# A decoder layer's expert stage: the input rows spread by transfers inside SBUF and turned by VectorE in 32x32 blocks, instead of turned by TensorE

## The reference, cut to what matters

```
logits = x @ router_weight.T + router_bias
top_val, top_idx = jax.lax.top_k(logits, 4)          # 4 of 16 experts for each token
gate_up = x @ gate_up_proj[e] + gate_up_proj_bias[e]  # 512 -> 512 gate, 512 up
gate = min(gate, 7); up = clip(up, -7, 7)
glu = gate * sigmoid(1.702 * gate)
out_e = ((up + 1) * glu) @ down_proj[e] + down_proj_bias[e]
out = sum over the 4 experts of weight * out_e;  x = layernorm(x + out)
```

## Time and profile before

| what | us |
|---|---|
| median of 3 runs (1515.5 to 1519.87) | 1516.45 |
| the profiled execution's own time | 1519.72 |
| its span, from the first to the last instruction | 1518.0 |
| PE busy | 1417.6 (93%) |
| DVE, ACT, POOL busy | 949.6, 725.7, 864.8 |
| the experts, from the first turned row to the last product | about 700 |

### The profile page before, as it was taken

How to read it: one execution, slowest core, us unless ns; L and a number is a source line. 1 busy time by engine, 2 the same in 40 slices (tenths; PEclk the granted TensorE clock), 3 DMA queues, 4 the chain that set the end, 5 groups by cost and what they waited for, 6 DMA issues and landing times. The chain is left out here.

```text
span 1518.0 us, 26960 instructions
## 1 busy us (share of the span) xinstructions
PE 1417.6 (93%) x7502; PEld 1016.7 (67%) x7502; DVE 949.6 (63%) x1425; ACT 725.7 (48%) x1405; POOL 864.8 (57%) x712
## 2 busy tenths in 40 slices
PE   6999999889999999998959999999999999999992
PEld 5878888534444444443347888888888888888882
DVE  2334234777888788789875655565656565656564
ACT  4212221268777877876624424444444444354233
POOL 4435342545586577655558456676667586377522
PEclk9999999989999999999869999999999999999996
DMA  5301003464666666571147456666656577375455
GB/s 200 92 22 52 14 26 49 75 111 66 114 118 90 134 130 91 121 128 46 67 160 213 102 125 161 168 163 157 166 142 169 135 202 171 71 195 141 73 129 173
DMA packets 93407, 180.84 MB, mean 119 GB/s; under 512 B 19064, under 2 KB 21880, under 8 KB 92248
## 3 DMA queue, kind: packets, MB, share of 16 engines
q1 hardware_dynamic: 73800, 133.04, 35.3%
q0 software_dynamic: 18320, 45.59, 16.0%
q10 hardware_dynamic: 1152, 0.52, 0.2%
HBM read 116.04 MB, written 33.47 MB: 98 GB/s over the span
## 5 line engine op out<-in xcount | busy, mean ns | idle before, releaser
L952 DVE TENSOR_REDUCE stage<-ps_a 128x2 f32<-128x1024 f32 x256 | 300.0, 1217 | 71.2 <-PE ps_a L1301 70.6
L750 ACT ACTIVATE probs<-ps_b 128x512 f32<-128x512 f32 x504 | 274.3, 596 | 51.6 <-PE ps_b L1316 47.0
L2090 POOL TENSOR_TENSOR we_split<-we_raw,we_split 128x512 f32 (+1 forms) x192 | 248.8, 1535 | 75.8 <-ACT we_split L2081 74.2
L2484 PE MATMUL ps_y<-we_split,hT 128*128 x900 | 226.2, 400 | 2.7 <-issue 1.6
L2484 PE MATMUL ps_u<-we_split,xT 128*128 x900 | 226.1, 400 | 0.0
L2484 PE MATMUL ps_g<-we_split,xT 128*128 x900 | 218.6, 392 | 0.5 <-POOL we_split L2090 0.5
L2484 PEld LDWEIGHTS ps_g<-we_split,xT 128*128 128x128 f32 x900 | 170.0, 189 | 36.3 <-issue 0.9
L2484 PEld LDWEIGHTS ps_y<-we_split,hT 128*128 128x128 f32 x900 | 164.7, 190 | 34.9 <-issue 3.4
L2230 POOL DMA_INDIRECT scratch_acc<-x_keep,to_rows x75 | 119.6, 1594 | 117.1 <-issue 64.2
L2484 PEld LDWEIGHTS ps_u<-we_split,xT 128*128 128x128 f32 x900 | 163.5, 188 | 32.8
L2290 ACT ACTIVATE hT<-ps_h 128x512 fp32r<-128x512 f32 x75 | 44.7, 595 | 292.8 <-PE ps_h L2456 292.8
(11 more groups left out here) (353 smaller groups left out, 2198.9 us busy)
## 6 DMA issues: line engine op xcount, KB each, us to landing
we_raw<-in_w_expert SPq DMA_DIRECT2D x180, 256.0 KB
stack<-xT_raw SPq DMA_DIRECT2D x192, 128.0 KB, 5.5
we_bias<-in_b_expert SPq DMA_DIRECT2D x16, 768.0 KB, 4.6
stage<-in_w SPq DMA_DIRECT2D x5, 1024.0 KB, 5.3
xT_raw<-in_xT SPq DMA_DIRECT2D x4, 1024.0 KB, 6.8
x_tok<-in_x POOLq DMA_DIRECT2D x16, 256.0 KB, 3.0
stage<-in_ctx SPq DMA_DIRECT2D x7, 512.0 KB, 5.5
late<-o_pair SPq DMA_DIRECT2D x112, 32.0 KB
```

What stands on the lines that cost most here:

```text
L750: nc.scalar.activation(probs[:, n % 3, h], src[:], ACT.Exp, scale=DH ** -0.5).then_inc(b_kept, 1)
L952: nc.vector.tensor_reduce(out[:, :, i, k % NC], ps_a[i][:], AX.X, ALU.max, negate=True).then_inc(a_kept[i], 1)
L2090: nc.gpsimd.tensor_tensor(lo, W["raw"][:, k, c], hi, ALU.subtract).then_inc(W["lo"], 1)
L2484: mm = nc.tensor.matmul(out[:], left[:, a, c], w[:, bass.ds(par, 1), k, b, c].squeeze(1), start=(n == 0), stop=(n == len(passes) - 1))
```

## The change

The rows of a tile are no longer turned by PE. ACT issues four transfers inside SBUF for each tile (`move_rows`): transfer q takes columns 128q to 128q+127 of all 128 gathered rows and writes them to the 32 partitions from 32q, four rows of 128 numbers to a partition. One VectorE instruction (`turn_x`) then turns every 32x32 block of that. The result holds the same numbers as a full transpose, but with the 512 input features in another order over (partition, chunk), so the weights of gate and up are loaded in that order too (`weight_rows`). `x_hi` and `x_lo` read the turned rows from SBUF, with a step, instead of from PSUM. PSUM bank `ps_x` and four instructions of PE for each tile go. The buffers for the final layer norm move to make room. Expert 0's weights come in 12 transfers instead of 3.

```diff
-                sp.dma_start(W["raw"][:, k], A["w_expert"][0][:, k]).then_inc(W["loaded"][k], 16)
+                for c in range(KC):
+                    sp.dma_start(W["raw"][:, k, c], weight_rows(A, 0, k, c)).then_inc(W["loaded"][k], 16)
...
+def weight_rows(A, e, k, c):
+
+    if k == 2:
+        return A["w_expert"][e][:, k, c]
+    return A["w_expert"][e][32 * c:32 * c + 32, k].rearrange("a q d -> q a d")
...
-            sp.dma_start(W["raw"][:, k, c], A["w_expert"][e][:, k, c]).then_inc(W["loaded"][k], 16)
+            sp.dma_start(W["raw"][:, k, c], weight_rows(A, e, k, c)).then_inc(W["loaded"][k], 16)
...
-    act.wait_ge(W["loaded"][k], 16 * KC * e + 16)
+    act.wait_ge(W["loaded"][k], 16 * KC * e + 16 * KC)
...
+        moved_rows, turned_rows = [x[:, U + i] for i in range(2)], x[:, U + 2]
+        by_quarter = turned_rows.rearrange("p (g c b) -> p c b g", g=4, c=KC)
...
-                nc.scalar.activation(xT[:, j % 2, 0], four(ps_x), ACT.Copy).then_inc(xT_hi, 1)
+                nc.scalar.activation(by_row(xT[:, j % 2, 0]), by_quarter, ACT.Copy).then_inc(xT_hi, 1)
+
+            def move_rows(i, j):
+                act.wait_ge(gathered[j], 16 * (i // U) + 16)
+                if i >= 2:
+                    act.wait_ge(x_turned, i - 1)
+                for q in range(4):
+                    act.dma_start(moved_rows[i % 2][32 * q:32 * q + 32, :], x_rows[j][:, q * P:q * P + P]).then_inc(
+                        moved[i % 2], 16)
...
             for j in range(2):
+                move_rows(j, j)
+            for j in range(2):
                 x_hi(j, j)
...
                 if i < TILES - 3:
                     aim_from(i + 3, (j + 3) % U)
+                if i < TILES - 2:
+                    move_rows(i + 2, (i + 2) % U)
                 new = act.value_load(pick(G["new"], i), min_val=0, max_val=1)
...
-                nc.vector.tensor_tensor(xT[:, j % 2, 1], four(ps_x), xT[:, j % 2, 0], ALU.subtract).then_inc(xT_lo, 1)
+                nc.vector.tensor_tensor(by_row(xT[:, j % 2, 1]), by_quarter, by_row(xT[:, j % 2, 0]),
+                                        ALU.subtract).then_inc(xT_lo, 1)
+
+            def turn_x(i):
+                dve.wait_ge(moved[i % 2], 64 * (i // 2) + 64)
+                if i > 0:
+                    dve.wait_ge(xT_lo, i)
+                nc.vector.transpose(turned_rows, moved_rows[i % 2]).then_inc(x_turned, 1)
...
                 nc.vector.scalar_tensor_tensor(h[:], ps_u[:], 1.0, glu[:], ALU.add, ALU.mult).then_inc(h_made, 1)
+                if i < TILES - 2:
+                    turn_x(i + 2)
                 if not is_at(i, 0):
                     finish(i - 1, (j - 1) % U)
...
-                if not (isinstance(i, int) and i >= TILES - 2):
-                    turn_x(i + 2, (j + 2) % U)
                 if not is_at(i, 0):
                     down(i - 1)
```

More of the change, by code:

```diff
@@ L2128, in bank @@
             return ctx.enter_context(nc.psum_tensor(name, [P, D], F32))
-        ps_g, ps_u, ps_x, ps_h, ps_y = bank("ps_g"), bank("ps_u2"), bank("ps_x"), bank("ps_h"), bank("ps_y")
+        ps_g, ps_u, ps_h, ps_y = bank("ps_g"), bank("ps_u2"), bank("ps_h"), bank("ps_y")
         from_set, to_set = sem("from_set"), sem("to_set")
@@ L2140, in experts @@
         added, weight_kept = sem("added"), sem("weight_kept")
[L2141 removed]
+        moved = [sem("moved0"), sem("moved1")]
+        final_step = sem("final_step")
         pair_loaded = [sem(f"pair_loaded{g}") for g in range(PAIRS)]
```

28 lines of the change are left out of this document (12 added, 16 removed).

## The result

The changed kernel takes **1735.22 us** (median of 4 runs, 1727.22 to 1744.02) against 1517.09 for the kernel before on the same chip: ratio 1.143, 95% interval 1.140 to 1.147. The prediction had the direction (slower, 0.91), but 1646 us and a range that ended at 1720. The profiled execution took 1732.96 us, with a span of 1731.3.

The account below looks back on a forecast made before the run. In the experts PE alone was taken to set the pace. Terms -26 + 91 + 34 + 31 = +130 on the profiled 1519.7 gave 1649.7, forecast as 1646 us against the runs' median; own range 1600 to 1700 (0.55), overall range 1570 to 1720.

Parts of the forecast that it names:

- Removed: -26 us: PE's row in each tile: one of two 0.35 us pieces goes, 75 times, -26 us; a tile takes 8.77 us.
- An ordinary tile pays 0: Ordinary tile: turn, later x_hi and four issues on ACT still let down start at 8.55, due 8.77; cost 0.
- Where an expert begins: 6.2 us: First three downs of an expert late by 2.1, 2.2 and 1.9 us, at 14 later beginnings and partly the first: +91 us.
- Its first part: First down of an expert: ACT's three weight copies start 2.6 us later behind x_hi, delaying h; 2.1 us lost.
- the other two: Second and third down of an expert: ACT waits for later gathers ahead of its issues and h; 2.2 and 1.9 us.
- The loads: +34 and +31: Gate and up loads on four DMA engines: +34 us for the first tile, +31 us at later experts.
- The second term: Later experts: loads last 43.4 us, so experts of 3 tiles lack 10.4 us and those of 4 lack 1.6; +31 us.
- x_lo against POOL: x_lo with both inputs in SBUF and POOL shut each other out; third down 2.2 us later, 1677 us; left out of sum.
- the first (1729 us): Rival: four engines are full everywhere, so the later-load term is 137 us; +213, 1729 us; chance 0.15.
- The second (moved rows late, 1691): Rival: moved rows land late and DVE waits before finish and x_hi; 0.6 us times 75, +45, 1691 us; chance 0.10.
- The third's 1586 us: Rival: all 16 engines carry gate and up, so nothing is late later; +70, 1586 us; chance 0.13.

Follow-up runs that it names:

- the kernel before with narrow loads: Kernel before, TensorE still turning rows, only gate and up loaded four rows outermost, then 32, as in the change: 1592.55 us.
- with x_lo out of the way: DVE writes turned rows to PSUM, where x_hi and x_lo read them: 1738.70 us against the changed kernel, 1605.25 with gate and up loaded 128 rows outermost.
- wide loads: Changed kernel with gate and up rows laid out by the host so their loads have 128 rows outermost again: 1669.88 us.
- the third buffer's kernel: Third moved-rows buffer added to wide loads, PSUM turned rows, gathers four tiles ahead, spread copies, moves behind h's cut: 1523.22 us; 1600.96 with four-engine loads.

## Why the prediction was wrong

**Removed: -26 us. Too small.** A quiet tile saves 0.47, 35 us in all: besides the 0.35 us of transposes, the step from ps_y to ps_g fell from 2.84 to 2.72 us.

**An ordinary tile pays 0. Right.** The issues took 0.62 us, x_hi stood 3.1 us behind ps_u's end (3.2), and quiet tiles ran at 8.65. The turn took 0.71 (0.68). x_hi took 1.14 us and not 0.6 to 0.7; a quiet tile covers that.

**Where an expert begins: 6.2 us. This is the step that failed.** Its first part held: 2.46 us at the first down (2.1 forecast), the moves' issues during the copies, the gather at 14.2 us behind ps_u's end (13.9). The mechanism of the other two held as well, ACT waiting for a gather. Their size did not. Where no weights are loaded all three held: at the last beginning PE idled 1.71, 2.52 and 1.64 us, where the forecast was 2.1, 2.2 and 1.9. But the step took a landing of 3.6 us from the earlier trace rows, where no weights were being loaded, for all 14. It was 7.2 us beside the narrow loads that the very next paragraph described, and 4.5 beside wide ones. It held moved rows to be in time by a landing from another stage; they were late 30 times, 73.8 us. And it priced gaps at their own length. The products behind them ran in part at the lower clock, 47 us in all. No row of before has an example in the experts, but the first row has the clock at 0.50 where PE was busy 6.58 of 20 us. Measured, the four periods from one ps_g to the next in which PE pays for a beginning are 11.7, 16.4, 9.1 and 11.8 us in the mean of the 14, instead of 8.65; at the last beginning alone they are 10.7, 11.4, 10.6 and 8.8.

**The loads: +34 and +31.** The first was near: ACT's last copy ended at 809.5 (808.1 forecast), start and first two tiles cost 40.7. DVE's first x_lo took 4.00 us, held by POOL. The second term was right in itself for experts of 3 tiles, as the kernel before with narrow loads shows (9.1 and 8.8 us against 10.4), not for those of 4, and came to nothing here, since each expert already lasts 11 to 14 us longer. The larger effect of the loads was left out: the transfers beside them are late. Without the start and the two tiles behind it, that is worth 38 us in the change and 103 us with x_lo out of the way. The number of engines that the prediction took from the Trainium skill (DMA: Bandwidth & Descriptors, "Why a DMA increments its semaphore by 16 and not by 1") agrees with the trace: q1 has 73560 packets and with wide loads 75096, which is 1536 more, 12 for each of the 128 loads of gate and up, as 16 closing packets against 4 make. SP's issue of a chunk, 328 ns in the median with wide loads, took 874 and up to 5342.

**x_lo against POOL: left out, "no row here shows the two side by side".** It was real. It held DVE for 7.9 to 9.1 us at six beginnings of the changed kernel, and nine times for 8.8 us and more with wide loads. The Trainium skill (SBUF — State Buffer, "SBUF: two separate sides") says that such a pair excludes each other for an instruction's whole length; here an x_lo waited for six of POOL's instructions, longer than that. It says too that the one that is issued first keeps the other out; with wide loads x_lo started 0.37 us ahead of the six and ended behind them. The estimate of 31 us was too low. Adding it would have given 1677, nearer but not for what happened: in the changed kernel the late gathers mostly hide it, and its price depends on what else is late. That x_lo took 1.09 us, as the 1.08 of the earlier trace rows had it, is luck. That row is the mean of two instructions of L999, of 0.69 and 1.48 us, and the longer one (at 761.68) overlaps a POOL instruction that runs from 761.11 to 762.61; no POOL instruction overlaps the other. So a row of before did show the two side by side, inside a mean, and two inputs in SBUF alone cost nothing.

**The sum**, as the trace has it: -35 for quiet tiles, +41 for the start, +142 for idle PE ahead of ps_y beyond the first, +47 for the lower clock, together +195 of the 213 us by which the profiled span grew; the other 18 are not placed. **The rivals:** the first (1729 us) came nearest, by luck: it had ACT waiting for weights throughout, and ACT waited for them in the first two experts alone. How full the four engines were, no view here shows. The second (moved rows late, 1691) was there with 73.8 us of waits. The third's 1586 us are for loads on all 16 engines: the run with wide loads took 1670, and 1605 with x_lo's wait taken away too. The mistake was to give these as alternatives, where late rows, the lower clock and the exclusion that was left out happened together.

What stays open: which of DVE and POOL gives way, and why; which step makes x_hi take 1135 ns, the input's or the output's; why transfers in other queues land later beside the narrow loads; and the rest of what these loads cost the third buffer's kernel.

## What to carry to other kernels

When an edit puts a transfer in front of work that used not to wait for it, take its landing from a stretch with the traffic that it will meet, not from a quiet one, and give it another tile of lead before anything else is tuned. A layout that leaves few rows outermost hurts not only its own transfer but those that run beside it, in other queues too. And where two waits end together, removing either can show nothing: test them in pairs before calling one harmless. A mean is no price either: look at the median before a slower instruction is put down to its operands.

## What the runs showed of the hardware that was not expected

- What a gap costs in clock, in the changed kernel: down's twelve products took 3.0 us behind each of the nine gaps of 0.9 to 1.8 us. Behind the nine gaps of 2.2 to 2.7 us they took 3.0 five times and 4.35 to 5.49 four times (granted clock 0.59, 0.66 and 0.62 in three of these); behind each of the twenty of 3.3 us and more, 4.36 to 5.48. The length of the gap alone does not decide it: in the kernel with wide loads, turned rows in PSUM and gathers four tiles ahead, they took 4.56 to 4.60 behind four gaps of 1.80 to 1.91 us, and 3.00 behind two of 1.93.
- x_lo on DVE took 0.68 us with one input in PSUM, 0.68 with both in SBUF and in order, 1.09 with one of them read out of SBUF with a step, and up to 9.5 us beside POOL's low halves. x_hi on ACT took 1.13 us out of SBUF and 0.60 out of PSUM with the same step.
- VectorE can turn 32x32 blocks from SBUF straight to PSUM, in 0.72 us for 128x512 against 0.70 to SBUF; that frees both readers.
- A gather of 128 rows landed 3.6 us after its start in a quiet stretch; beside wide loads of weights in 3.5 to 5.9 (median 3.9), beside loads on four engines in up to 7.8 (median 5.4).
